# Two-layer graph convolution on one core: weight copies to ScalarE, small tables ahead of the edges, sign rows to GpSimd

## The reference

```python
def gcn_conv(x, W, b, src, dst, n):
    h = x @ W
    deg = zeros(n).at[dst].add(1.0) + 1.0
    dinv = rsqrt(deg)
    norm = dinv[src] * dinv[dst]
    agg = segment_sum(h[src] * norm[:, None], dst, num_segments=n)
    return agg + h * (dinv * dinv)[:, None] + b
h = gcn_conv(emb, W1, b1, src, dst, NTOKEN)          # emb 18750x64, W1 64x128
nodes = gcn_conv(h, W2, b2, src, dst, NTOKEN)        # W2 128x64
out = nodes[input.reshape(-1)].reshape(b_, l_, NINP)
```

## Time and profile before

| | |
|---|---|
| median of 3 runs | 3978.09 us (3972.21 to 3984.72) |
| profiled execution | 3968.11 us, its span 3966.3 us |
| busy share of the span | PE 72%, DVE 76%, ACT 34%, POOL 43% |
| mean granted TensorE clock | 0.865 of full speed |
| instructions | 75,858 |

### The profile page before, as it was taken

The page is one execution under the profiler, slowest core; times in us unless marked ns, Lnnn a source line. Parts: engine busy times, 40 slices in busy tenths (PEclk is TensorE's granted clock), DMA queues, the critical chain, the costliest instruction groups (busy, mean ns, idle before and its releaser), DMA issues.

```text
span 3966.3 us, 75858 instructions
## 1 busy us (share of the span) xinstructions
PE 2859.6 (72%) x28219; PEld 2560.2 (65%) x28219; DVE 3020.1 (76%) x8786; ACT 1349.7 (34%) x3172; POOL 1688.4 (43%) x1565
## 2 busy tenths in 40 slices
PE   7996544421377888998988885888888878788661
PEld 6884223210367778888878785877777767777551
DVE  8999999999577897888878884767677666666440
ACT  6774212210333333443433341333333323333220
POOL 1000000000355555656556544556565566666535
PEclk9997566655589999999999997999899889989875
DMA  3000000001123223333333334344444223323211
GB/s 78 0 0 4 24 8 16 16 8 2 50 71 89 71 73 80 88 89 82 89 77 86 80 75 134 106 122 127 116 128 127 77 72 76 76 71 77 60 49 18
DMA packets 223188, 267.01 MB, mean 67 GB/s; under 512 B 117633, under 2 KB 130177, under 8 KB 222574
## 3 DMA queue, kind: packets, MB, share of 16 engines
q1 hardware_dynamic: 173132, 189.10, 16.4%
q0 software_dynamic: 49728, 73.53, 9.5%
HBM read 210.85 MB, written 51.88 MB: 66 GB/s over the span
## 4 chain that ended last, share of the span: by engine, by line
PE 48%; DVE 34%; another core or an unknown queue 9%; issue 4%; ACT 2%; POOL 1%; SPq 1%; DMA 1%; DVEq 0%; POOLq 0%; ACTq 0%
PE ps L1134 17%; PE ps L1199 17%; PE ps L1019 8%; DVE oh L1774 8%; DVE keys L1449 6%; DVE keys L1450 6%; DVE keys L1679 4%; DVE zoh L1758 2%; PE ps L1165 2%; ACT steps_oh L980 1%; PE ps L1170 1%; PE ps L1085 1%; DVE arena L1685 1%; DVE keys L1464 1%
## 5 line engine op out<-in xcount | busy, mean ns | idle before, releaser
L829 POOL DMA_INDIRECT zring<-table,sidx x1298 | 1417.5, 1092 | 1086.1 <-PE ps L1165 590.0
L1134 PE MATMUL ps<-arena,keys 128*128 128x192 bf16 x11472 | 1330.7, 255 | 382.8 <-issue 189.2
L980 ACT ACTIVATE steps_oh<-ps 128x384 bf16<-128x384 f32 x1912 | 921.6, 490 | 1866.5 <-PE ps L1134 1282.8
L1199 PE MATMUL ps<-steps_oh,oh 128*128 128x192 bf16 x11466 | 1320.3, 253 | 2.3 <-issue 2.3
L1134 PEld LDWEIGHTS ps<-arena,keys 128*128 128x128 bf16 x11472 | 1006.9, 101 | 451.8 <-issue 271.8
L1774 DVE TENSOR_SCALAR oh<-io_h,dl 128x384 bf16<-128x384 int16 x3822 | 986.9, 319 | 96.7 <-remote 66.4
L1199 PEld LDWEIGHTS ps<-steps_oh,oh 128*128 128x128 bf16 x11466 | 1021.7, 101 | 15.7 <-issue 4.3
L1679 DVE TENSOR_SCALAR keys<-keys,lanes 128x1024 bf16<-128x1024 int16 x1434 | 612.0, 481 | 15.6 <-DMA keys<-srel 11.4
L1758 DVE TENSOR_SCALAR zoh<-io_h,dl 128x128 bf16<-128x128 int16 x1064 | 243.7, 264 | 411.0 <-remote 226.8
L749 POOL DMA_INDIRECT arena<-line,row_i x16 | 16.5, 1029 | 1001.2 <-DVEq L1520 997.0
L1085 PE MATMUL ps<-ident,keys 128*128 128x128 f32 x464 | 98.0, 402 | 313.3 <-DVE keys L1450 308.4
(11 more groups left out here) (263 smaller groups left out, 1699.3 us busy)
## 6 DMA issues: line engine op xcount, KB each, us to landing
keys<-srel SPq DMA_DIRECT2D x478, 256.0 KB
out<-res SPq DMA_DIRECT2D x50, 512.0 KB
zring<-table,sidx POOLq DMA_INDIRECT x1298
table<-arena SPq DMA_DIRECT2D x19, 384.0 KB, 2.8
table<-sgn_l SPq DMA_DIRECT2D x39, 144.0 KB
nodes<-arena SPq DMA_DIRECT2D x39, 96.0 KB
arena<-in_L_rec_edge_index SPq DMA_DIRECT2D x2, 1171.5 KB, 6.5
arena<-nodes,oidx POOLq DMA_INDIRECT x108
```

What stands on the lines that cost most here:

```text
L829: pool.indirect_dma_start(out=zring[:, i % RING, :], out_offset=None, in_=rows_of, in_offset=bass.IndirectOffsetOnAxis(ap=sidx[:, col:col ...
L980: act.activation(grow[:, j % 2, h * 2 * ROW:(h + 1) * 2 * ROW], pg[h][:, 0:2 * ROW], ACT.Copy).then_inc(evac, 1)
L1134: mm = pe.matmul(pg[t // 2][:, t % 2 * ROW:(t % 2 + 1) * ROW], s_oh[:, j // 2 % 2, k, e:e + P], xtab[:, (w * WIN + k) * ROW:(w * WIN + k + ...
L1199: mm = pe.matmul(sums(sl, k), dwin[:, j % 2, t, k * P:(k + 1) * P], grow[:, j % 2, t * ROW:(t + 1) * ROW], start=False, stop=(w == CELLS - ...
```

## The change

ScalarE gets the three copies on the way to the products and the three behind them; `b1r` is now filled with 1.0 and then scaled by b1, not filled with 0.0 and then added to. TensorE waits for them by `w_turned` and `w_made`. VectorE's block of the cells' tables and the parity moves from behind the keys to ahead of the wait for the edges, unchanged. The five operations on the sign rows go to GpSimd, behind its iotas and ahead of all its gathers; it waits for the parity (`parity`) and for its own iotas, and VectorE waits for the fifth (`signs`) before it inverts the roots.

```diff
 @block.gpsimd (behind the iotas)
+            pool.wait_ge(parity, 1)
+            pool.wait_ge(iotas, 5 + SB - 6)
+            pool.tensor_scalar(sgn_t[:, 6, :], sgn_t[:, 6, :], odd[:, 0:1], None, ALU.add).then_inc(signs, 1)
+            pool.wait_ge(signs, 1)
+            for n, sgn in enumerate((sgn_t[:, 6:7, :], sgn_l)):
+                pool.tensor_scalar(sgn[:, :, :], sgn[:, :, :], 1.0, -2.0, ALU.is_equal, ALU.mult).then_inc(signs, 1)
+                pool.wait_ge(signs, 2 * n + 2)
+                pool.tensor_scalar(sgn[:, :, :], sgn[:, :, :], 1.0, None, ALU.add).then_inc(signs, 1)
 @block.scalar (at its start)
+            act.wait_ge(setup_mm, 1)
+            act.wait_ge(w_in, 64)
+            act.activation(w1t[:, 0:F], psum[6][:, 0:F], ACT.Copy).then_inc(w_turned, 1)
+            act.activation(w1t[:, F:2 * F], psum[6][:, 0:F], ACT.Copy).then_inc(w_turned, 1)
+            act.activation(b1r[:, :], b1r[:, :], ACT.Copy, scale=b1s[:, 0:1]).then_inc(w_turned, 1)
+            act.wait_ge(setup_mm, 3)
+            act.activation(w12[0:F, 0:F], psum[5][0:F, 0:F], ACT.Copy).then_inc(w_made, 1)
+            act.activation(w12[F:2 * F, F:2 * F], psum[5][F:2 * F, 0:F], ACT.Copy).then_inc(w_made, 1)
+            act.activation(c12[:, :], psum[4][:, 0:F], ACT.Copy).then_inc(w_made, 1)
             act.wait_ge(nlo_ready, 1)
 @block.tensor
             pe.transpose(psum[6][:, 0:F], w1s[:, :], ident[0:F, 0:F]).then_inc(setup_mm, 1)
-            pe.wait_ge(const, 3)
+            pe.wait_ge(w_turned, 3)
...
+            pe.wait_ge(w_made, 3)
             pe.wait_ge(hist_oh, 1)
             count_start(psum[5])
 @block.vector
-            dve.memset(b1r[:, :], 0.0)
+            dve.memset(b1r[:, :], 1.0)
...
-            dve.wait_ge(setup_mm, 1)
-            dve.wait_ge(w_in, 64)
-            dve.tensor_copy(w1t[:, 0:F], psum[6][:, 0:F])
-            dve.tensor_scalar(b1r[:, :], b1r[:, :], b1s[:, 0:1], None, ALU.add)
-            link(dve.tensor_copy(w1t[:, F:2 * F], psum[6][:, 0:F]))
-            dve.sem_inc(const, 1)
-            dve.wait_ge(setup_mm, 3)
-            dve.tensor_copy(w12[0:F, 0:F], psum[5][0:F, 0:F])
-            dve.tensor_copy(w12[F:2 * F, F:2 * F], psum[5][F:2 * F, 0:F])
-            link(dve.tensor_copy(c12[:, :], psum[4][:, 0:F]))
...
             (the cells' tables, L1366 to L1383, stand here now, ahead of dve.wait_ge(edge_in, 64))
-            dve.wait_ge(iotas, 5 + SB - 6)
-            link(dve.tensor_scalar(sgn_t[:, 6, :], sgn_t[:, 6, :], odd[:, 0:1], None, ALU.add))
-            for sgn in (sgn_t[:, 6:7, :], sgn_l):
-                link(dve.tensor_scalar(sgn[:, :, :], sgn[:, :, :], 1.0, -2.0, ALU.is_equal, ALU.mult))
-                link(dve.tensor_scalar(sgn[:, :, :], sgn[:, :, :], 1.0, None, ALU.add))
+            dve.sem_inc(parity, 1)
...
+            dve.wait_ge(signs, 5)
             dve.wait_ge(root, 1)
             link(dve.reciprocal(dinv[:, :], nwt[:, :]))
...
+            dve.wait_ge(w_made, 3)
             for layer in range(2):
```

More of the change, by code:

```diff
@@ L348, in gcn_program @@
         setup_mm = sem("setup_mm")
+        w_turned = sem("w_turned")
+        w_made = sem("w_made")
+        signs = sem("signs")
+        parity = sem("parity")
         node_tr = sem("node_tr")
@@ L1313, in _ @@
             dve.sem_inc(const, 1)
-            dve.wait_ge(setup_mm, 1)
-            dve.wait_ge(w_in, 64)
-            dve.tensor_copy(w1t[:, 0:F], psum[6][:, 0:F])
-            dve.tensor_scalar(b1r[:, :], b1r[:, :], b1s[:, 0:1], None, ALU.add)
-            link(dve.tensor_copy(w1t[:, F:2 * F], psum[6][:, 0:F]))
-            dve.sem_inc(const, 1)
-            dve.wait_ge(setup_mm, 3)
-            dve.tensor_copy(w12[0:F, 0:F], psum[5][0:F, 0:F])
-            dve.tensor_copy(w12[F:2 * F, F:2 * F], psum[5][F:2 * F, 0:F])
-            link(dve.tensor_copy(c12[:, :], psum[4][:, 0:F]))
+            cc = cell[:, :]
+            link(dve.tensor_scalar(group[:, :], cc, 669.0, None, ALU.mult))
+            link(dve.tensor_scalar(group[:, :], group[:, :], 15, None, ALU.logical_shift_right))
+            link(dve.scalar_tensor_tensor(out=cell_f[:, :], in0=group[:, :], scalar=-float(CELLS), in1=cc, op0=ALU.mult, op1=ALU.add))
+            note(dve.tensor_scalar(base[:, :], cell_f[:, :], float(WIN * P), None, ALU.mult))
+            link(dve.tensor_scalar(bound[:, :], cell_f[:, :], float(WIN), 256.0, ALU.mult, ALU.add))
+            link(dve.scalar_tensor_tensor(out=bound[:, :], in0=group[:, :], scalar=256.0, in1=bound[:, :], op0=ALU.mult, op1=ALU.add))
+            link(dve.tensor_scalar(bound[:, GT:GT + 1], it_y[:, 0:1], float(P // 2), float((ZB0 * P + ZOFF) // 2), ALU.mult, ALU.add))
+            note(dve.tensor_scalar(minus[:, :], bound[:, :], -1.0, 0.5, ALU.mult, ALU.add))
+            note(dve.tensor_copy(lowest[:, :], bound[:, :]))
+            link(dve.tensor_scalar(behind[:, 0:GT], bound[:, 0:GT], float(WIN), None, ALU.add))
+            link(dve.tensor_scalar(behind[:, GT:GT + 1], bound[:, GT:GT + 1], float(P // 2), None, ALU.add))
+            note(dve.tensor_scalar(lowest[:, :], lowest[:, :], 16, None, ALU.logical_shift_left))
+            link(dve.tensor_scalar(behind[:, :], behind[:, :], 16, None, ALU.logical_shift_left))
+            link(dve.memset(bad[:, :], 0.0))
+            link(dve.tensor_scalar(odd_i[:, :], it_y[:, 0:1], 1, None, ALU.bitwise_and))
+            link(dve.tensor_copy(odd[:, :], odd_i[:, :]))
+            dve.sem_inc(parity, 1)
             dve.wait_ge(edge_in, 64)
```

## The result

The changed kernel takes 3998.16 us in the median of ten runs (3980.57 to 4018.46) and the kernel before 3980.6 us (3962.79 to 3988.9). The ratio is 1.0043, with a 95% interval from 1.0023 to 1.0062: the change costs 17.6 us between the medians, where 7.3 us were to be gained. The profiled execution has a span of 3985.7 us, 19.4 us above that of before. The time lies outside the range of the prediction.

The account below looks back on a forecast made before the run. VectorE was taken to set the pace from the first edge work to the sort's end. Head 1.06, tables 2.67 and signs 3.54 sum to 7.27 us, taken off the median 3978.09: 3970.8 us, range 3963 to 3987.

Parts of the forecast that it names:

- The head: Before the edges: VectorE starts on them at 14.6 instead of 15.66 us, 1.06 us gained.
- Its bound: Head's gain: zero if the loads land a microsecond later, 2.6 us if both land as fast as the first.
- Cover of 4.3 us for the tables: In the head: VectorE's wait from 10.2 to 14.5 us hides the moved tables, which otherwise cost 2.67 us.
- ScalarE's part: Weight copies in the head: ScalarE is 0.6 us slower, but 2.6 and 6.6 us of cover make the cost zero.
- The tables: Between the sort keys and the roots: the cells' tables and parity leave VectorE, 2.67 us gained.
- The signs: Before the sort: five sign operations leave VectorE for GpSimd, 3.54 us gained unless VectorE then waits for them.
- I take zero, by the row that is nearest: Beside the one-hots: GpSimd's passes slow VectorE by nothing, as the iotas did; otherwise 10.3 to 34.8 us of standing.
- Cost as a wait: zero, with over 200 us of cover: Before the sort: the passes end between 50 and 145 us, VectorE asks for the signs only at 360.7 us.
- the first two rivals: First: reading passes stall VectorE in the one-hots, 3981, 3987 or 4006 us, chance 0.25; second: VectorE holds up GpSimd, 0.07.
- The second rival: One-hots keep the passes out until 340.5 us; at the mean rate VectorE waits 14.7 us, 3985.4 us; chance 0.07.
- The price of the passes: GpSimd's five sign passes, 9,600 elements a partition: 10.3 to 105 us, 16 us by the median iota.
- That the gain or loss before the sort reaches the end: Behind the sort: what follows moves with it; the opposing rival, 3978 us, had chance 0.08.

Follow-up runs that it names:

- e9: The changed kernel run again without edit on another chip: ratio 1.0065, 3511.22 against 3492.51 us for the kernel before.
- e12: Changed kernel with the sign operations on ScalarE instead of GpSimd, third run of that version: ratio 0.9987, 3486.1 against 3490.67 us.
- e8: Kernel before with only the cells' tables moved ahead of the weight copies, parity left in place: one run, 3923.21 against 3931.02 us.
- e1: Changed kernel with the five sign operations back on VectorE: ratio 0.9994, 3483.16 against 3485.73 us for the kernel before.
- e3: Changed kernel with the sign operations on ScalarE behind its square root, none on GpSimd: ratio 0.9994 to the kernel before.
- e11: Changed kernel with a GpSimd memset and a copy of it added ahead of the sign passes: one run, 3508.48 against 3490.67 us.
- e7: Changed kernel with each long GpSimd sign pass cut into nine pieces of 512 elements: one run, 3967.77 against 3931.02 us.
- e4: Changed kernel with VectorE's wait for the signs moved ahead, right behind the counts: one run, 3502.10 against 3485.73 us.
- e2: Kernel before with only the sign operations on GpSimd and the parity's two steps in the head: ratio 1.0053, 3503.24 against 3485.73 us.
- e6: Changed kernel with the three short sign passes run on GpSimd in the head, before the one-hots: one run, 3939.33 against 3931.02 us.

## Why the prediction was wrong

The head: 1.06 us predicted, 1.15 measured. Its bound was right too: in other runs the edges released VectorE between 14.23 us (e9) and 15.97 us (e12), so on some executions the head gives nothing. Cover of 4.3 us for the tables: 4.2 measured (10.28 to 14.51 us).

ScalarE's part: cost zero, right, though its first table load moved onto this way.

The tables: 2.67 us, right (e8 shows the 2.29 of it without the parity, e1 the whole).

The signs, 3.54 us taken from VectorE: right, and shown in e3.

The step that failed is the one on what the passes do to VectorE beside them: "I take zero, by the row that is nearest". VectorE stood for 25.54 us. With it fell "Cost as a wait: zero, with over 200 us of cover": the passes were to end between 50 and 145 us and ended at 371.03 us, behind the 360.7 us at which VectorE was to ask for them. The nearest row was of iotas, which only write; e11 shows that writing and reading differ on just this point. It went as a mixture of the first two rivals. As in the second, the one-hots kept the passes out until 340.4 us, not the other way round; the iotas had passed, since they don't read. As in the first, the passes then shut out VectorE, but behind the count and not in it. The second rival had counted only VectorE's wait at the end (14.7 us at the mean rate, none at the median) and took for granted that the making of the keys would run beside the passes.

The price of the passes was too small as well. By the median iota I put 1.67 ns an element; the long passes took 15.74 and, alone, 11.86 us for 4,608 elements, 3.4 and 2.6 ns, nearer to the mean iota (3.6 ns) that I kept as a bound. VectorE stood 1.72 us less than the first long pass took (14.02 of 15.74), since it met it 1.58 us after its start, and 0.34 us less than the second takes alone (11.52 of 11.86). With 7.7 us for each, the 1.67 ns of the prediction, that would be 6.0 + 7.3 = 13.3 us of standing and 6.0 us of loss, an estimate; on the 3980.6 us that is 3986.6, just inside the range. With the measured price it is 18.2. So both errors were needed to leave the range.

The page "SBUF — State Buffer" of the Trainium skill, section "Who interferes with whom", was set beside the row as a rule against the change. On reads and writes it agrees with the runs: 0.20 us for the memset, 300.56 for the copy. On who stands, that the second waits for the whole of the first, it agrees for the long passes, 14.26 and 12.90 us of VectorE. But the two that stood, L1379 and L1386, have one input in SBUF and not two, so the rule as the prediction took it, for instructions with two inputs, would have let them pass; the same section has a line of its own on `tensor_scalar`. In e7 it is not the whole instruction: VectorE stood 0.28 us beside a piece of 1.50 us. That a gapless stream keeps the other out for 301 us is more than the page says, which speaks of one instruction.

The page "GPSIMD Engine Reference" of the Trainium skill, section "Performance versus the Vector engine", gave 1.03 cycles an element and from it an estimate of 4 us for a long pass. The runs show 11.86 and 15.74 us in e4, where VectorE stood in its wait but for the three short instructions on the counts; the measurement decides.

That the gain or loss before the sort reaches the end was right: 18.1 us at the marker, 19.4 at the end of the span, 17.6 between the medians.

Two small slips in the working change nothing: 0.2 us is the longest of TensorE's 86 waits in the earlier trace rows, their mean is 14.8 / 86 = 0.17 us, and 360.7 - 340.5 is 20.2, not 20.1.

## What to carry to other kernels

An engine that seems idle is not free for work that another engine can keep out. Before work that reads SBUF is moved to GpSimd, look at what VectorE does from the moment it is issued until it must be done. Here VectorE made one-hots without a gap, the work started only behind them (340.4 us), and then it was VectorE that stood, for 25.54 us. A row of the trace is evidence only for an instruction that touches memory in the same way; an iota said nothing about a pass that reads. ScalarE had time at the right moment and took the same passes beside VectorE without slowing it (4.1 us each where GpSimd needs 12 to 16).

## What the hardware showed that was not expected

A gapless stream of VectorE instructions with two inputs in SBUF kept a reading GpSimd instruction out for as long as it lasted: 301.03 us for an instruction of 0.61 us, with no effect on the stream itself. Two inputs are not needed for standing: the second long pass, begun beside the one-input L1385, took 12.95 us for 11.86, and L1379 and L1386, with one input each, stood for 14.02 and 11.52 us. No run has a gapless stream of such instructions.

VectorE's instructions that take input from PSUM ran beside a long pass at their usual 0.31 us, three of them in each of five traces (the changed kernel, e2, e4, e6, e9).

GpSimd's simple passes over bf16 are slow: for 4,608 elements 15.74 us with two operations and 11.86 with one, where VectorE took 1.36 us for each and ScalarE 4.12 us.

The layers behind the sort took 2,940 us on one chip (1045.5 us to the end, changed kernel) and 2,457 us on another (e9), with the same instructions and the same first 1,040 us. The granted clock differs little between 1,200 and 2,000 us (0.96 and 0.97 against 0.99 and 1.00) and more between 2,400 and 2,800 us (0.87 against 0.99), where the two executions stand at different places of their work. What makes the difference was not tried.
